# Attention scores taken per head in row tiles and mixed after a trip through DRAM, in place of mixing the queries ahead of the scores

## The chip, the cores and the metric

The kernel runs on one core of a Trainium2 chip. Times are device microseconds of one launch; a launch works through the whole batch of 128 images. The engines are TensorE (PE in the rows; its weight loads are PEld), VectorE (DVE), ScalarE (ACT), GpSimd (POOL) and SyncE (SP), which issues all DMAs here. Less is better.

## The reference, cut to what matters

An image has 384 channels on 14x14 = 196 pixels. After a group normalisation and three 1x1 convolutions there are 8 heads with 32 query and key channels each and 128 value channels each. What the change touches is the talking-heads attention:

```python
attn = jnp.einsum('bhid,bhjd->bhij', q, k) * SCALE        # 8 heads, 196 x 196
attn = attn + ab[:, BIAS_IDXS][None]
attn = jnp.einsum('bhij,gh->bgij', attn, th1w) + _c(th1b)  # mix the heads
attn = jax.nn.softmax(attn, axis=-1)
attn = jnp.einsum('bhij,gh->bgij', attn, th2w) + _c(th2b)  # mix them again
o = jnp.einsum('bhij,bhjd->bhid', attn, v)
o = o.transpose(0, 1, 3, 2).reshape(Bb, DH, RES, RES) + vl # vl: 3x3 depthwise conv of v
o = jax.nn.relu(o)
return conv1x1_bn(o, pw, pb, p_s, p_t)                     # 1024 -> 384 channels
```

The result is added to x. All is float32.

## The kernel before, in words

The batch is worked off in 64 pairs of images. Every engine has one program, written out by hand in its order; `rounds` runs `step` for the first pair, in a loop over the 62 pairs between, and for the last pair. Semaphores tie the engines together; `wait_ge(s, n)` waits until semaphore s has reached n. The projection of one pair to the output lies in the step of the next pair.

Two kinds of matmul occur. `split3` takes operands that were split into a high and a low part and does three matmuls in the one-pass format float32r (low weights by high data, high by low, high by high). Plain float32 matmuls are one instruction in the program and two matmuls (with two weight loads) in the trace.

TensorE does in a step, in this order: 12 tiles `qkv_tile` (values 0 and 1, queries 0 and 1, keys 0 and 1, values 2 to 7) of nine float32r matmuls 128x392, which alternate between the two banks of `psA` and are taken out by ScalarE (`values`, `query_or_key`); projection tiles 0 and 1 of the pair before (`project`, 24 matmuls each); the scores; projection tile 2; the second mixing of the heads (14 uses of `mix_bank`, 4 float32 matmuls each, with `probs` as weights and `mixw` as data); and attention by values (32 float32 matmuls 128x196, image 0 first, then image 1).

The first mixing is folded into the queries: for each of the 8 mixed heads g, ScalarE multiplies the 256 query channels by th1w[g, h] (`mixed_high`, 16 a pair, written to `q_hi`), and VectorE makes the low part (`mixed_low`, 16 a pair, `q_lo`). ScalarE and GpSimd split the keys too (`key_high`, `k_hi`, `k_lo`). One query row of 14 pixels then gives 8 x 14 = 112 weight columns, and the logits of a step are 28 rows x 2 channel tiles x 3 = 168 float32r matmuls of 196 columns, in 14 groups of two rows, each in one of the four banks of `psL` and `psM` (`logit_bank`). VectorE adds the bias and takes the row's greatest value (28 times), ScalarE takes the exponential and the sum (28 times), VectorE the reciprocal of the sums once per image (`rinv`), and GpSimd scales the second mixing matrix by it (`mixing_weights`, four instructions per image).

The values are turned by VectorE (`turn`), go to DRAM in eight DMAs (`turned_out`), come back by key in four (`keys_in`), and are put in the order of the heads by ScalarE (`head_major`, four copies). VectorE's remaining time goes to the depthwise convolution (64 instructions `conv` a pair, dealt out by `convs(count)`), to the adds of convolution and attention (8) and to the low halves of the projection's input (`low`, 8).

## Time and profile before

| what | value |
|---|---|
| median of 3 runs | 4535.83 us (4534.75 to 4536.31) |
| the profiled execution | 4534.58 us |
| its span, first to last instruction | 4532.8 us |
| PE busy | 4505.5 us, 99% |
| DVE busy | 4197.4 us, 93% |
| ACT busy | 3570.3 us, 79% |
| POOL busy | 1360.9 us, 30% |
| one pair in the middle of the run | 70.26 us |
| DMA share of 16 engines | 27.3%, 356 MB in all |

The span is 1.8 us below the profiled execution's time, which is 1.3 us below the median. A busy share says how long an engine had an instruction in it; matmuls are pipelined, so their listed lengths overlap, and what one costs is read from the distance of two starts or from a stretch divided by their count.

### The profile page before, as it was taken

The numbers are of one execution on the slowest core, as the hardware profiler recorded it, in microseconds if no ns is written. First come the engines' busy times: TensorE is split into PE (matmuls) and PEld (weight loads), VectorE is DVE, ScalarE is ACT, GpSimd is POOL, SyncE is SP. The second block draws the span as 40 slices with busy tenths as digits, with TensorE's granted clock in tenths as the row PEclk, the third lists the DMA queues.
The fourth block names the chain that finished last, engine by engine and source line by source line (L and its number), as shares of the span: only waits on it lengthen the run. The fifth ranks groups of instructions, "written<-read, shape, count | busy, mean of one in ns | idle before, by whom it ended". The sixth has DMA issues, their size and how long they took to land.

```text
span 4532.8 us, 108461 instructions
## 1 busy us (share of the span) xinstructions
PE 4505.5 (99%) x33666; PEld 4502.5 (99%) x33666; DVE 4197.4 (93%) x10015; ACT 3570.3 (79%) x8508; POOL 1360.9 (30%) x1288
## 2 busy tenths in 40 slices
PE   7999999999999999999999999999999999999999
PEld 7999999999999999999999999999999999999999
DVE  8999999999999999999999999999999999999998
ACT  7787877878778787787787877878778778787786
POOL 2323323323233232332322323323233232332322
PEclk9999999999999999999999999999999999999999
DMA  3322222223222232222322322223222232232222
GB/s 94 97 65 81 86 69 87 65 81 92 70 81 74 72 97 65 81 82 68 93 65 81 88 72 82 68 78 97 65 81 79 67 97 65 81 86 68 88 65 76
DMA packets 211502, 356.05 MB, mean 79 GB/s; under 512 B 15843, under 2 KB 132691, under 8 KB 211413
## 3 DMA queue, kind: packets, MB, share of 16 engines
q1 hardware_dynamic: 211478, 355.75, 27.3%
q8 instruction: 13, 0.21, 0.0%
q14 instruction: 11, 0.09, 0.0%
HBM read 199.71 MB, written 155.98 MB: 78 GB/s over the span
## 4 chain that ended last, share of the span: by engine, by line
PE 99%; DMA 0%; POOL 0%; DVE 0%; SPq 0%; ACT 0%; issue 0%; POOLq 0%; DVEq 0%
PE psA L293 45%; PE psA L426 15%; PE psL L293 13%; PE psM L293 10%; PE psM L404 9%; PE psL L404 7%; PE psA L306 0%; DMA qa<-in_wqkv 0%; SPq L254 0%; POOL xs L822 0%; DVE probs L730 0%; DMA by_key<-probs 0%; POOL wp_lo L863 0%; DVE q_lo L722 0%; ACT w_hi L443 0%
## 5 line engine op out<-in xcount | busy, mean ns | idle before, releaser
L700 DVE SCALAR_TENSOR_TENSOR psC<-vpad,par,psC 128x406 f32<-128x406 f32 x3072 | 1807.2, 635 | 0.0
L584 ACT ACTIVATE probs<-probs,nmax 112x196 f32<-112x196 f32 x1792 | 803.2, 451 | 128.8 <-DVE nmax L759 112.9
L293 PE MATMUL psA<-x_hi,w_lo 128*128 128x392 f32 x2304 | 794.9, 345 | 6.0 <-DVE x_lo L679 6.0
L293 PE MATMUL psA<-x_hi,w_hi 128*128 128x392 f32 x2304 | 785.7, 341 | 0.0
L293 PE MATMUL psA<-x_lo,w_hi 128*128 128x392 f32 x2304 | 785.1, 341 | 0.0
L426 PE MATMUL psA<-qa,shared 105*128 105x196 f32 x4096 | 690.9, 329 | 0.0
L426 PEld LDWEIGHTS psA<-qa,shared 105*128 105x128 f32 x4096 | 677.2, 190 | 0.4 <-DVE shared L794 0.3
L857 POOL TENSOR_TENSOR k_lo<-qk,k_hi 128x392 fp32r<-128x392 f32 x128 | 159.9, 1249 | 1636.4 <-ACT k_hi L490 1636.4
L722 DVE SCALAR_TENSOR_TENSOR q_lo<-qk,th,q_hi 128x392 fp32r<-128x392 f32 x1024 | 618.3, 632 | 2.0 <-ACT q_hi L486 1.9
L486 ACT ACTIVATE q_hi<-qk,th 128x392 fp32r<-128x392 f32 x1024 | 594.5, 618 | 2.1
L461 ACT ACTIVATE o_hi<-shared 128x392 fp32r<-128x392 f32 x512 | 271.6, 530 | 391.3 <-DVE shared L794 391.3
L293 PE MATMUL psL<-k_hi,q_lo 128*112 128x196 f32 x2048 | 534.4, 261 | 5.3 <-DVE q_lo L722 4.2
L293 PE MATMUL psL<-k_lo,q_hi 128*112 128x196 f32 x2048 | 536.2, 262 | 0.0
L293 PE MATMUL psL<-k_hi,q_hi 128*112 128x196 f32 x2048 | 535.9, 262 | 0.0
L293 PE MATMUL psA<-o_hi,wp_lo 128*128 128x392 f32 x1536 | 526.6, 343 | 0.0
L293 PE MATMUL psA<-o_lo,wp_hi 128*128 128x392 f32 x1536 | 523.1, 341 | 0.0
L293 PE MATMUL psA<-o_hi,wp_hi 128*128 128x392 f32 x1536 | 521.0, 339 | 0.0
L844 POOL TENSOR_TENSOR mixw<-kron,rinv 112x448 f32<-112x448 f32 (+1 forms) x512 | 455.9, 921 | 135.5 <-DVE rinv L773 123.3
L510 ACT ACTIVATE vpad<-psA,par 128x392 f32<-128x392 f32 x512 | 349.5, 683 | 141.6 <-PE psA L293 135.0
L700 DVE SCALAR_TENSOR_TENSOR psC<-vpad,par,shared 128x406 f32<-128x406 f32 x512 | 327.4, 661 | 143.0 <-ACT shared L456 143.0
L293 PEld LDWEIGHTS psA<-x_hi,w_lo 128*128 128x128 f32 x2304 | 434.3, 189 | 6.4 <-issue 6.4
L404 PE MATMUL psM<-mixw,probs 113*105 113x112 f32 x4096 | 435.9, 260 | 4.6 <-POOL mixw L844 4.6
(85 smaller groups left out, 10723.1 us busy)
## 6 DMA issues: line engine op xcount, KB each, us to landing
by_key<-probs SPq DMA_DIRECT2D x512, 224.0 KB, 3.6
qa<-by_key SPq DMA_DIRECT2D x128, 448.0 KB, 4.3
qk<-by_key SPq DMA_DIRECT2D x128, 448.0 KB, 6.9
xs<-in_x SPq DMA_DIRECT2D x64, 588.0 KB, 3.8
shared<-in_x SPq DMA_DIRECT2D x64, 588.0 KB, 3.8
out<-shared SPq DMA_DIRECT2D x63, 588.0 KB, 3.0
qa<-in_wqkv SPq DMA_DIRECT2D x3, 768.0 KB, 7.1
stage_wp<-in_wp SPq DMA_DIRECT2D x1, 1536.0 KB, 9.6
```

Source lines behind the costliest of these rows:

```text
L293: last = nc.tensor.matmul(dst, w, r, start=(begin and n == 0), stop=(end and n == 2))
L404: mm = nc.tensor.matmul(bank[:, jc, :, b, :], probs[0:HP + 1, img, 2 * n + b, jc * HALF:(jc + 1) * HALF], mixw[0:HP + 1, img, 2 * n + b, : ...
L426: mm = nc.tensor.matmul(psA[:, u % 2, e * PIX:(e + 1) * PIX], vt[0:HALF, img, jc, g * D:(g + 1) * D], attn[:, img, jc, g, :], start=(jc == ...
L461: nc.scalar.activation(o_hi[:, 2 * n:2 * n + 2, img * PIX:(img + 1) * PIX], acc[:, 2 * n:2 * n + 2, img * IMG:img * IMG + PIX], ACT.Relu). ...
L486: nc.scalar.activation(q_hi[dst], src, ACT.Copy, scale=th1[:, kt, g:g + 1]).then_inc(s_qhi, 1)
L510: nc.scalar.activation(dst[:, :, 0:RES, 0:RES], psA[:, m % 2, 0:COLS].rearrange("p (i r w) -> p i r w", i=2, w=RES), ACT.Identity, bias=qk ...
L584: nc.scalar.activation(row, row, ACT.Exp, bias=nmax[:, img, b:b + 1], scale=-1.0, accum_out=rowsum[:, img, b:b + 1]).then_inc(s_exp, 1)
L700: nc.vector.scalar_tensor_tensor(a if tap == 7 else sums, src, taps[:, c, TAPS[tap]:TAPS[tap] + 1], a if tap == 0 else sums, MUL, ADD).the ...
L722: nc.vector.scalar_tensor_tensor(q_lo[dst], src, th1[:, kt, g:g + 1], q_hi[dst].bitcast(f32), MUL, SUB).then_inc(s_qlo, 1)
L844: nc.gpsimd.tensor_tensor(mixw[0:HP, img, b0:b0 + nb, :], k2, rinv[:, img, b0:b0 + nb].unsqueeze(2).broadcast_to([HP, nb, HP]), MUL).then_ ...
L857: nc.gpsimd.tensor_tensor(k_lo[:, kt, :], k[:, kt, :], k_hi[:, kt, :].bitcast(f32), SUB).then_inc(s_klo, 1)
```

## The change

The queries are no longer mixed ahead of the scores. A pair's scores are taken per head, in 4 units of 98 query pixels (7 query rows of 14; two units per image). For a unit `head_scores` issues 8 float32 matmuls with only 32 partitions of weights and data each: r is the quarter of the partitions that a head's 32 channels lie in, and the four quarters write to the four banks of `psL` and `psM`. The units stand on TensorE's queue behind value tiles 2, 3, 4 and 5. ScalarE copies two banks and VectorE two banks of each unit into `scores`; SP stores the unit to DRAM (`scores_out`) and loads it back with one partition per head and pixel column (`heads_in`) into `by_head`: 8 transfers a pair. The first mixing is then one float32 matmul of 392 columns for two query rows, 14 a pair, with the constant matrix `kron1` as weights. These stand in fours ahead of the projection tiles. The splits of queries and keys and the weight table `th1` go away. The order of attention by values becomes image by image within each pair of heads and starts only when all 14 mixing uses were copied; ReLU is done twice (once into `o_hi`, once in place); six of the eight low halves go to GpSimd, and so do two of the four `head_major` copies.

```diff
+        scores = qa[0:UNIT, :].rearrange("p (i c h n) -> p i c h n", i=2, c=2, h=NH)
+        turned = qa[:, 0:TURNED].rearrange("p (i b c n) -> p i b c n", i=2, b=BLOCKS, c=VT)
+        head_rows = nc.dram_tensor("head_rows", (4, NH, UNIT, PIX), f32, kind="Internal").ap()
+        raw = [v.rearrange("p (j n) -> p j n", j=2) for v in (qa[:, TURNED:TURNED + 2 * DH], qk_room[:, 0:2 * DH])]
...
-        def mixed(kt, g):
-
-            return ((slice(None), slice(None), kt, slice(g * RES, (g + 1) * RES)),
-                    q[:, kt, :].rearrange("p (b i) -> p b i", i=RES))
-
+        def score_bank(r):
+
+            return (psL if r < 2 else psM)[:, r % 2, 0:2 * PIX]
+
+        UNITS = [(img, c) for img in range(2) for c in range(2)]
...
+            def scores_out(t, u):
+
+                img, c = UNITS[u]
+                sp.wait_ge(s_score_a, 8 * t + 2 * u + 2)
+                sp.wait_ge(s_score_v, 8 * t + 2 * u + 2)
+                sp.dma_start(head_rows[u].rearrange("h i j -> i h j"), scores[0:UNIT, img, c, :, :]
+                             ).then_inc(s_score_out[u], 16)
+
+            def heads_in(t, u):
+
+                img, c = UNITS[u]
+                sp.wait_ge(s_score_out[u], 16 * (t + 1))
+                sp.dma_start(by_head[:, img, c * ROWS_B * PIX:(c + 1) * ROWS_B * PIX],
+                             head_rows[u].rearrange("h (w b) j -> (h w) (b j)", w=RES)).then_inc(s_moved[u], 16)
...
-                turned_out(t)
-                ones_in(t)
-                keys_in(t)
+                if first:
+                    sp.wait_ge(s_bias, 1)
+                else:
+                    wait_alone(sp, s_olo, 6 * t)
+                    wait_alone(sp, s_olo_v, 2 * t)
+                    wait_alone(sp, s_av_mm, 8 * t)
+                scores_out(t, 0)
+                scores_out(t, 1)
+                heads_in(t, 0)
+                scores_out(t, 2)
+                heads_in(t, 1)
+                scores_out(t, 3)
+                heads_in(t, 2)
+                heads_in(t, 3)
+                turned_out(t, 0)
+                turned_out(t, 1)
+                keys_in(t, 0)
+                keys_in(t, 1)
...
+            def head_scores(t, first, u):
+
+                img, c = UNITS[u]
+                if u:
+                    pe.wait_ge(s_score_a, 8 * t + 2 * u)
+                    pe.wait_ge(s_score_v, 8 * t + 2 * u)
+                else:
+                    pe.wait_ge(s_qk_sb, 4 * t + 4)
+                    if not first:
+                        pe.wait_ge(s_mix_sb, 14 * t)
+                at_ = (2 * img + c) * UNIT
+                for kt in range(QT):
+                    for r in range(QUADS):
+                        part_ = slice(r * KD, (r + 1) * KD)
+                        mm = nc.tensor.matmul(score_bank(r)[0:UNIT, kt * PIX:(kt + 1) * PIX],
+                                              q[part_, kt, at_:at_ + UNIT],
+                                              k[part_, kt, img * PIX:(img + 1) * PIX], start=True, stop=True)
+                mm.then_inc(s_score_mm, 1)
...
+                    if m < 6:
+                        head_scores(t, first, m - 2)
                 if first:
                     pe.wait_ge(s_v_sb, VT)
-                else:
-                    project(t, 0, True)
-                    project(t, 1, True)
-
-                pe.wait_ge(s_klo, 2 * (t + 1))
-                pe.wait_ge(s_qlo, 16 * (t + 1))
...
+                    if n == 0:
+                        pe.wait_ge(s_score_a, 8 * t + 8)
+                        pe.wait_ge(s_score_v, 8 * t + 8)
+                    if n % 7 == 0:
+                        pe.wait_ge(s_moved[2 * img], MOVES * (t + 1))
+                    if n % 7 == 3:
+                        pe.wait_ge(s_moved[2 * img + 1], MOVES * (t + 1))
...
-                    elif not first:
-                        pe.wait_ge(s_mix_sb, 14 * (t - 1) + 11 + n)
-                    for b in (b0, b0 + 1):
-                        for kt in range(QT):
-                            px = slice(img * PIX, (img + 1) * PIX)
-                            mm = split3(logit_bank(n)[:, (b - b0) * PIX:(b - b0 + 1) * PIX],
-                                        q_lo[:, img * RES + b, kt, :], q_hi[:, img * RES + b, kt, :],
-                                        k_lo[:, kt, px], k_hi[:, kt, px], kt == 0, kt == QT - 1)
-                    mm.then_inc(s_logit_mm, 1)
+                    nc.tensor.matmul(logit_bank(n)[:, 0:2 * PIX], kron1[:, :, :].rearrange("p g i -> p (g i)"),
+                                     by_head[:, img, b0 * PIX:(b0 + 2) * PIX], start=True, stop=True
+                                     ).then_inc(s_logit_mm, 1)
...
+                    if n in (3, 7, 11) and not first:
+                        if n == 7 and not last:
+                            pe.wait_ge(s_gs, t + 2)
+                        project(t, n // 4, True)
+
+                if first:
...
                 for img in range(2):
-                    pe.wait_ge(s_vt_sb, 4 * t + 2 * img + 2)
-                    pe.wait_ge(s_mix_sb, 14 * t + 7 * img + 7)
-                    for n in range(4):
-                        u = 4 * img + n
-                        if u >= 2:
-                            pe.wait_ge(s_add, 8 * t + u - 1)
...
+                    pe.wait_ge(s_vt_sb[img], 2 * (t + 1))
+                pe.wait_ge(s_mix_sb, 14 * t + 14)
+                for u in range(8):
+                    n, img = divmod(u, 2)
+                    if u >= 2:
+                        pe.wait_ge(s_add, 8 * t + u - 1)
...
-            def relu(t, img, n):
-                act.wait_ge(s_add, 8 * t + 4 * img + n + 1)
-                nc.scalar.activation(o_hi[:, 2 * n:2 * n + 2, img * PIX:(img + 1) * PIX],
-                                     acc[:, 2 * n:2 * n + 2, img * IMG:img * IMG + PIX], ACT.Relu).then_inc(s_relu, 1)
...
+            def relu(t, u):
+                n, img = divmod(u, 2)
+                act.wait_ge(s_add, 8 * t + u + 1)
+                a = acc[:, 2 * n:2 * n + 2, img * IMG:img * IMG + PIX]
+                nc.scalar.activation(o_hi[:, 2 * n:2 * n + 2, img * PIX:(img + 1) * PIX], a, ACT.Relu).then_inc(s_relu, 1)
+                nc.scalar.activation(a, a, ACT.Relu).then_inc(s_relu, 1)
...
-            def mixed_high(t, kt, g):
-                act.wait_ge(s_qk_sb, 4 * t + kt + 1)
-                dst, src = mixed(kt, g)
-                nc.scalar.activation(q_hi[dst], src, ACT.Copy, scale=th1[:, kt, g:g + 1]).then_inc(s_qhi, 1)
-
-            def key_high(t, kt):
-                act.wait_ge(s_qk_sb, 4 * t + kt + 3)
-                nc.scalar.copy(k_hi[:, kt, :], k[:, kt, :]).then_inc(s_khi, 1)
-
-            def head_major(t, img, jc):
-                act.wait_ge(s_raw[img], 32 * (t + 1))
-                nc.scalar.copy(vt[0:HALF, img, jc, :].rearrange("p (c a n) -> p c a n", c=VT, a=QUADS),
-                               raw[img][0:HALF, jc, :].rearrange("p (a c n) -> p c a n", a=QUADS, c=VT)
-                               ).then_inc(s_vt_sb, 1)
...
+            def head_major(t, jc):
+                act.wait_ge(s_raw[1], 32 * (t + 1))
+                nc.scalar.copy(vt[0:HALF, 1, jc, :].rearrange("p (c a n) -> p c a n", c=VT, a=QUADS),
+                               raw[1][0:HALF, jc, :].rearrange("p (a c n) -> p c a n", a=QUADS, c=VT)
+                               ).then_inc(s_vt_sb[1], 1)
...
+                for u in range(4):
+                    values(2 + u)
+                    score_copy(t, u, 0)
+                    score_copy(t, u, 1)
+                    if u < 2:
+                        conv_centre(t, first, u + 2)
+                    elif not last:
+                        stat(t + 1, 0, u - 2)
...
-                CENTRES = {1: 4, 3: 5, 9: 6, 11: 7}
+                CENTRES = {8: 4, 11: 5, 23: 6, 25: 7}
...
+                    if n == 3 and not last:
                         group_moments(t + 1)
                     if n in CENTRES:
-                        conv_centre(t, CENTRES[n])
+                        conv_centre(t, first, CENTRES[n])
+                    if n in (7, 15) and not first:
+                        projected(t, n // 8)
                 if not first:
                     projected(t, 2)
...
+                    if use == 0:
+                        act.wait_ge(s_vt_out[0], OUTS * (t + 1))
+                        act.wait_ge(s_vt_out[1], OUTS * (t + 1))
+                        act.wait_ge(s_moved[2], MOVES * (t + 1))
                     if use == 7:
-                        act.wait_ge(s_vt_sb, 4 * t + 2)
+                        act.wait_ge(s_moved[3], MOVES * (t + 1))
+                        act.wait_ge(s_vt_sb[0], 2 * (t + 1))
...
-                    if use in COPIES:
-                        head_major(t, *COPIES[use])
-                    if use == 6 and not last:
+                    if use in (3, 6):
+                        head_major(t, use // 4)
+                if not first:
+                    act.wait_ge(s_proj_mm, 3 * t)
+                for u in range(8):
+                    relu(t, u)
+                    if u == 0 and not last:
                         act.wait_ge(s_v_mm, VT * (t + 1))
                         x_high(t + 1)
...
+                def score_copies(u):
+                    img, c = UNITS[u]
+                    dve.wait_ge(s_score_mm, 4 * t + u + 1)
+                    for r in (2, 3):
+                        nc.vector.tensor_copy(scores[0:UNIT, img, c, r:NH:QUADS, :],
+                                              score_bank(r)[0:UNIT, :].rearrange("p (k n) -> p k n", k=QT)
+                                              ).then_inc(s_score_v, 1)
...
+                convs(14)
+                if first:
+                    dve.wait_ge(s_wlo, CT)
+                for u in range(4):
+                    score_copies(u)
+                    convs(2 if u < 3 else 3)
...
+                    if n in (3, 7):
+                        turn(n // 4)
+                        convs(3)
+                    if n == 11:
+                        convs(7)
...
+            def head_major(t, jc):
+
+                if jc == 0:
+                    wait_alone(pool, s_logit_mm, 14 * t + 11)
+                wait_alone(pool, s_raw[0], 32 * (t + 1))
+                nc.gpsimd.tensor_copy(vt[0:HALF, 0, jc, :].rearrange("p (c a n) -> p c a n", c=VT, a=QUADS),
+                                      raw[0][0:HALF, jc, :].rearrange("p (a c n) -> p c a n", a=QUADS, c=VT)
+                                      ).then_inc(s_vt_sb[0], 1)
...
                 mixing_weights(t, first, 0)
+                head_major(t, 0)
+                head_major(t, 1)
                 mixing_weights(t, first, 1)
                 if not first:
                     residual(t, 2)
```

TensorE's queue at the end of the projection tiles and the start of the logits, kernel before (x_hi, o_hi and the like are high parts, the second name is the weight):

```order
L293 MATMUL psA<-o_hi,wp_hi 128x392
L369 REGISTER_ALU
L370 REGISTER_ALU [waits s_klo]
L376 ISA [waits s_qlo]
L293 MATMUL psL<-k_hi,q_lo 112x196 [waits s_mix_sb]
L293 MATMUL psL<-k_lo,q_hi 112x196
L293 MATMUL psL<-k_hi,q_hi 112x196
```

The logits follow behind projection tile 1 and wait for the split keys and queries. In the changed kernel the first of four groups of scores stands right behind value tile 2:

```order
L371 REGISTER_ALU [waits s_qk_sb]
L376 MATMUL psL<-qk_room 98x196 [waits s_mix_sb]
L376 MATMUL psL<-qk_room 98x196
L376 MATMUL psM<-qk_room 98x196 x2
L376 MATMUL psL<-qk_room 98x196 x2
L376 MATMUL psM<-qk_room 98x196 x2
L320 MATMUL psA<-x_hi,w_lo 128x392 [waits s_qk_sb]
```

It waits for the last key tile, and value tile 3 follows. The logits of the changed kernel stand behind value tile 7; projection tile 0 (L320, o_hi) follows behind the fourth:

```order
L420 REGISTER_ALU [waits s_score_v,s_score_a]
L425 MATMUL psL<-shared,kron 112x392 [waits s_moved0]
L425 MATMUL psL<-shared,kron 112x392
L425 MATMUL psM<-shared,kron 112x392
L429 REGISTER_ALU
L430 REGISTER_ALU [waits s_v_sb]
L333 MATMUL psA<-mv,same 128x4 [waits s_stat]
L425 MATMUL psM<-shared,kron 112x392 [waits s_moved1]
L339 REGISTER_ALU
L346 ISA [waits s_v_sb]
L320 MATMUL psA<-o_hi,wp_lo 128x392 [waits s_olo]
```

What was 12 matmuls a group is one, and the waits are now for the loads back from DRAM (s_moved0, s_moved1). SP's queue in the loop, before, behind the load of x:

```order
L254 DMA by_key<-probs 32x7x256 [waits s_turned]
L254 DMA by_key<-probs 32x7x256 x7
L259 REGISTER_ALU
L260 DMA probs<-in_ones 1x3584 [waits s_vt_out]
L264 REGISTER_ALU
L267 DMA qa<-by_key 112x1024 [waits s_logit_mm]
L267 DMA qa<-by_key 112x1024
L267 DMA qk<-by_key 112x1024 x2
```

And in the changed kernel, at the same place, with L262 `scores_out` and L269 `heads_in`:

```order
L262 DMA head_rows<-qa 98x8x196 [waits s_score_v,s_score_a]
L260 REGISTER_ALU
L262 DMA head_rows<-qa 98x8x196 [waits s_score_v,s_score_a]
L268 REGISTER_ALU
L269 DMA shared<-head_rows 112x1372 [waits s_score_out0]
L260 REGISTER_ALU
L262 DMA head_rows<-qa 98x8x196 [waits s_score_v,s_score_a]
L269 DMA shared<-head_rows 112x1372 [waits s_score_out1]
L260 REGISTER_ALU
L262 DMA head_rows<-qa 98x8x196 [waits s_score_v,s_score_a]
L269 DMA shared<-head_rows 112x1372 [waits s_score_out2]
L269 DMA shared<-head_rows 112x1372 [waits s_score_out3]
```

The eight stores of the turned values, which were first, follow behind the last of these rows.

## Rows read from the trace of the kernel before

**Rows 1.** Windows, one pair by stage: length, busy (x instructions) per engine, PEclk, DMA share, GB/s

```profile
1985.88:2005.30 19.42, 19.42 (x111) 19.42 (x109) 16.76 (x29) 16.07 (x28) 2.50 (x2) 1.00 0.00 0
2005.30:2013.87 8.57, 8.57 (x49) 8.57 (x49) 8.57 (x14) 7.87 (x17) 0.00 (x0) 1.00 0.42 97
2013.87:2030.60 16.73, 16.73 (x171) 16.73 (x170) 16.41 (x69) 14.66 (x55) 10.17 (x10) 1.00 0.21 61
2030.60:2034.92 4.32, 4.32 (x27) 4.31 (x26) 4.32 (x12) 1.71 (x8) 2.36 (x4) 1.00 0.75 221
2034.92:2045.65 10.73, 10.73 (x113) 10.73 (x112) 10.73 (x21) 10.21 (x18) 6.18 (x6) 1.00 0.63 194
2045.65:2056.14 10.49, 10.49 (x66) 10.49 (x65) 8.59 (x17) 5.18 (x10) 0.00 (x0) 1.00 0.19 57
1985.88:2056.14 70.26, 70.26 (x528) 70.24 (x527) 65.39 (x157) 55.69 (x134) 21.20 (x20) 1.00 0.27 78
```

**Rows 2.** The page, part 1: busy time and share of the span

```profile
PE 4505.5 (99%) x33666; PEld 4502.5 (99%) x33666; DVE 4197.4 (93%) x10015; ACT 3570.3 (79%) x8508; POOL 1360.9 (30%) x1288
```

**Rows 3.** Groups of PE by form: busy us, mean ns of one | idle before

```profile
L426 PE MATMUL psA<-qa,shared 105*128 105x196 f32 x4096 | 690.9, 329 | 0.0
```

**Rows 4.** Timeline of PE: start us, length us, instruction (merged rows as x)

```profile
2017.40 0.30 PE L306 MATMUL psA<-mv,same 128*128 128x4 f32 x2
2017.56 0.33 PE L293 MATMUL psM<-k_hi,q_lo 128*112 128x196 f32 x1
...
2056.14 0.48 PE L293 MATMUL psA<-x_hi,w_lo 128*128 128x392 f32 x1
2056.46 0.34 PE L293 MATMUL psA<-x_lo,w_hi 128*128 128x392 f32 x1
2056.64 0.34 PE L293 MATMUL psA<-x_hi,w_hi 128*128 128x392 f32 x1
```

**Rows 5.** Timeline of ACT in the attention-mixing stage

```profile
2038.03 0.97 ACT L601 COPY qa<-psL 105x448 f32<-105x448 f32 x2
...
2045.36 1.03 ACT L601 COPY qa<-psM 105x448 f32<-105x448 f32 x2
```

**Rows 6.** Groups of DVE by form

```profile
L722 DVE SCALAR_TENSOR_TENSOR q_lo<-qk,th,q_hi 128x392 fp32r<-128x392 f32 x1024 | 618.3, 632 | 2.0 <-ACT q_hi L486 1.9
...
L794 DVE TENSOR_TENSOR shared<-psA,shared 128x392 f32<-128x392 f32 x512 | 289.6, 566 | 140.0 <-PE psA L426 140.0
```

**Rows 7.** Groups of ACT by form

```profile
L584 ACT ACTIVATE probs<-probs,nmax 112x196 f32<-112x196 f32 x1792 | 803.2, 451 | 128.8 <-DVE nmax L759 112.9
L486 ACT ACTIVATE q_hi<-qk,th 128x392 fp32r<-128x392 f32 x1024 | 594.5, 618 | 2.1
...
L461 ACT ACTIVATE o_hi<-shared 128x392 fp32r<-128x392 f32 x512 | 271.6, 530 | 391.3 <-DVE shared L794 391.3
L601 ACT COPY qa<-psM 105x448 f32<-105x448 f32 x512 | 263.3, 557 | 24.5 <-PE psM L404 18.8
...
L494 ACT COPY shared<-qa 105x1024 f32<-105x1024 f32 x128 | 135.4, 1058 | 0.0
```

**Rows 8.** Groups of POOL by form

```profile
L844 POOL TENSOR_TENSOR mixw<-kron,rinv 112x448 f32<-112x448 f32 x384 | 389.4, 1041 | 135.5 <-DVE rinv L773 123.3 <-DVE rinv L769 12.2
...
L827 POOL TENSOR_TENSOR x_lo<-xs,x_hi 128x1176 fp32r<-128x1176 f32 x63 | 169.7, 2694 | 255.1 <-ACT x_hi L439 255.1
```

**Rows 9.** The page, part 6: DMA issues, KB each, us to landing

```profile
by_key<-probs SPq DMA_DIRECT2D x512, 224.0 KB, 3.6
qa<-by_key SPq DMA_DIRECT2D x128, 448.0 KB, 4.3
```

**Rows 10.** Timeline of SP's queue: the eight stores of the turned values

```profile
2009.29 6.30 SPq L254 DMA_DIRECT2D by_key<-probs  x8
```

**Rows 11.** Windows of the value stores and of the loads back, columns as in Rows 1

```profile
2009.00:2018.50 9.50, 9.50 (x76) 9.49 (x75) 9.37 (x27) 7.79 (x22) 0.00 (x0) 1.00 0.74 193
2030.80:2041.00 10.20, 10.20 (x88) 10.19 (x88) 10.20 (x24) 7.06 (x17) 5.65 (x7) 1.00 0.80 238
```

292 lines of the change are left out of this document (118 added, 174 removed).

## Prediction

> **What bounds the kernel now.** I read the page's busy shares first: PE 99%, DVE 93% [rows 2]. A share alone would not decide it, so I cut one pair of the middle of the run into TensorE's stages with the windows view [rows 1]. In each of the six stages PE is busy for the whole stretch, at full granted clock, and the stages add up to the pair: 19.42 + 8.57 + 16.73 + 4.32 + 10.73 + 10.49 = 70.26 us. DVE is busy 65.39 us of it, ACT 55.69, POOL 21.20. So the time of the pair is what stands on TensorE's queue, and the other engines hide behind it. 64 pairs of 70.26 are 4497 us; the other 36 are the start, and the projection of the last pair. Below, T is the time since the pair's first value tile (1985.88 in the trace). The projection begins at T = 19.42, the second mixing (10.73) at 49.04, attention by values at 59.77.
>
> **What leaves TensorE.** The logits stretch, 16.73 us. The two small group-sum matmuls in it stay; they take 0.16, from one start to the next [rows 4]. That leaves 16.57 us, or 0.0986 per float32r matmul of 196 columns (168 of them).
>
> **What comes, the mixing.** A float32 matmul shows as two, each over twice the columns' time: attention by values has 32 in the code and 64 per pair in the trace (4096 of 64 pairs, [rows 3]), in 10.49 us [rows 1], 0.164 each at 196 columns. The new mixing has 14 matmuls of 392 columns, 28 halves of 2 x 0.164 = 0.328: 9.18 us.
>
> **What comes, the scores.** 32 float32 matmuls of 196 columns are 64 halves. No row shows matmuls on 32 partitions, so the cost is bounded by the nearest row, the same 0.164. If the four quarters of the array do not overlap at all: 64 x 0.164 = 10.49. If four run abreast all the time: 2.62. The code's order decides between them. The quarters follow one another, but each matmul's two halves use the same quarter, so the second half has to wait for the first; if starts stay in the queue's order, the next quarter starts only with that second half. Then two run abreast: 9 steps of 0.164 a unit, 1.48, and 5.90 a pair. I take this one. No row here shows either.
>
> The array changes eight times a pair between whole and quarters. Unseen too: at least nothing, at most about 0.37 a change, the difference of a matmul's listed length and its pitch (0.34 - 0.18 [rows 4]) plus a load of some 0.2. I take 0.14, what the pitch grows by when PE goes from attention to the split matmuls (56.14 to 56.46 is 0.32, the next pitch 0.18, [rows 4]): 1.12. The same 0.14 three times for the returns from the mixing's groups to the projection: 0.42. "TensorEngine Tiling (Array Packing)", Key Properties, in the Trainium skill says that a change of tiling mode drains the engine; the price is left open there.
>
> The sum on TensorE: 9.18 + 5.90 + 1.12 + 0.42 = 16.62 in, 16.57 out. **The work is a draw**; what decides is the new waits.
>
> **Wait 1, ahead of attention by values.** Before, image 0 needed only the first seven copied mixing uses, and attention began where the mixing ended [rows 1]. Now it waits for the copy of the last use. ScalarE's copies follow each other in about 0.49 (two in 0.97 to 1.03, [rows 5], 0.557 alone [rows 7]); with the hand-over on both sides I take 0.65. Nothing is left on PE's queue to cover it.
>
> **Wait 2, in the mixing.** Projection tile 2 stood between the logits and the mixing; now the last two logit groups come behind it, and mixing use 0 follows them directly. ScalarE still has the last four exponentials (0.451 each), one convolution centre and the copy of tile 2 ahead of its first mixing copy, some 3.3 us after the last group, while PE has four banks = 3.07 us of mixing before it needs one back. Then two `head_major` copies of 1.058 [rows 7] stand in the first seven uses. I take 0.4.
>
> **Wait 3, the scores' trip through DRAM.** A tile takes 19.42 / 12 = 1.62. Value tile 2 is the seventh and ends at T = 11.3, unit 0 some 1.6 later, at 12.9; it is copied at 14.0 (two copies of 0.56 each on ScalarE and VectorE, [rows 6, 7]). A unit is 98 x 8 x 784 bytes = 615 KB each way. The stores of the turned values, in runs of 1 KB, moved 193 GB/s at 0.74 of the engines, so 261 at full share; the loads back, in runs of 4 KB, 238 at 0.80, so 298 [rows 11]. With runs of 784 bytes and 98 partitions I estimate 2.9 us a store, and 2.1 a load, each with about 1.3 until the semaphore (a 224 KB store lands after 3.6, a 448 KB load after 4.3, [rows 9]; issuing one takes SP 6.30 / 8 = 0.79, [rows 10]). Up to the load of unit 1, which the fourth logit group waits for, the queue moves out 0, out 1, in 0, out 2, in 1: 14.5 + 2.9 + 2.9 + 2.1 + 2.9 + 2.1 + 1.3 = 28.7. PE gets there at 19.42 + 7.02 + 2.1 = 28.5. I take 0.3. Units 2 and 3 land by about 36, and their groups are due at 35 and 41, behind projection tiles. So this wait is the floor under any speed-up of the scores: each microsecond that they save brings PE to the fourth group earlier, and the transfers come hardly earlier.
>
> **What lies under cover.** VectorE loses 16 x 0.632 and six `low`, and gains 8 copies of about 0.57: some 9 us freed, off the path. ScalarE loses 16 x 0.618 and two `head_major`, gains 8 copies and 8 ReLUs of 0.530 [rows 7]: slightly less than before. Both have room in the pair's 70 us. `x_high` moves behind the first ReLU: ready 4.2 us after attention starts, x_lo (2.694, [rows 8]) at 6.9, needed at 10.49. If that cover went, the next pair's first tile would be late by the excess. The eight value stores move behind the scores' transfers and behind the second `turn`; they come back by T = 48, and attention needs them at 60.
>
> **Sum.** 0.05 + 0.65 + 0.4 + 0.3 = +1.4 us a pair; x 64 = +90. From the profiled execution's 4534.6 that is **4624 us**, 1.9% slower. Its own range, with the switch between 0 and 0.37 and the waits between half and double, is 4500 to 4715.
>
> **Rivals.**
> 1. Four abreast, but the floor binds: scores 2.62 instead of 5.90, the fourth group due at T = 25.3 and fed at about 28.1. 1.4 - 3.3 + 2.5 = +0.6 a pair: 4573. For it: the order of starts is only assumed. Chance 0.13.
> 2. **The other side: faster.** Four abreast, and the transfers quick enough (the DMA engines are idle at share 0.00 in the first 19 us, [rows 1]): 1.4 - 3.3 - 0.3 = -2.2 a pair: 4394. It decides when scores, changes and wait 3 together stay below 5.9 us instead of my 7.3. Against it: 1.9 MB of stores and loads between T = 14 and 28. Chance 0.18.
> 3. No overlap of the quarters: 10.49 instead of 5.90, wait 3 gone, +5.7 a pair: 4899. Chance 0.12.
> 4. GpSimd late: `head_major` of image 0 stands ahead of image 1's mixing weights on its queue and waits for the load back. If a copy of 1024 elements goes like x_lo (2.694 for 1176), two take 4.7, from T = 48 to 53, then the first weights 1.041 [rows 8]; use 7 is due at 55. A load 2.5 us later costs +1.5: 4720. Chance 0.12.
>
> **How the numbers follow.** The forecast has 0.45; of it 0.06 falls below the time before and 0.05 within 0.2% of it, about what a measurement of this kernel can tell from no change. Faster: 0.18 + 0.06 + 0.03 of rival 1 = 0.27; same: 0.05 + 0.04 = 0.09; slower 0.64. The range goes from rival 2's middle, 4395, to 4800 above rival 4: out stay rival 3 (0.12) and rival 2's better half.
>
> **What would show it.** The starts of the L376 matmuls: 0.164 between a quarter's halves and the next quarter's start with the second half; a unit near 1.5 us (0.7 or 2.7 in the rivals). Mixing halves at 0.328. PE's waits by name: the fourth logit group on the load of unit 1, attention's first matmul on ScalarE's last copy, mixing uses 4 and 7. PE's share falls to some 98%. Wrong it would be if DMA waits stand at other groups, or if ScalarE holds up value tiles 3 to 5 (2.5 us of its work a unit against 3.1 on PE).

## The result, and the profile after

| kernel | median, us | span of the profiled execution, us |
|---|---|---|
| before | 4535.29 (4 runs) | 4532.8 |
| changed | 4592.5 (4587.41 to 4595.26, 4 runs) | 4593.4 |

The changed kernel takes 1.0125 times as long, 95% interval 1.0113 to 1.0137: 57 us more. The forecast was 4624, range 4395 to 4800. (Of the experiments, one has only two timed runs: two others were disturbed and are left out.)

The page of the changed kernel, part 1 and the DMA queue of part 3 (packets, MB, share of 16 engines):

```profile
PE 4377.9 (95%) x28802; PEld 3920.6 (85%) x28802; DVE 3787.2 (82%) x9120; ACT 3322.5 (72%) x8252; POOL 1661.4 (36%) x1672
q1 hardware_dynamic: 448262, 669.57, 51.0%
```

Against [rows 2], TensorE has less to do (4377.9 us instead of 4505.5) in a longer span; VectorE and ScalarE have less too. No engine is full. So the question is what TensorE waits for. Its waits in the changed kernel, the view of who waited for whom (total us, times, longest), of which the kernel before had none that came back every pair:

```profile
PE psM L425 <- DMA shared<-head_rows: 87.4, 65, 2.1
PE psM L449 <- ACT qa L635: 42.5, 64, 1.8
PE psA L471 <- ACT qa L635: 40.0, 64, 0.7
PE psA L320 <- DVE shared L818: 20.3, 64, 0.4
PE psA L333 <- DVE mv L691: 7.0, 1, 7.0
PE psA L320 <- DVE x_lo L714: 5.9, 1, 5.9
PE psL L425 <- DVE nmax L778: 3.8, 2, 2.9
```

The first four come once a pair: 1.37 us for the load of unit 1 at the fourth logit group, 0.66 in the second mixing for ScalarE's copies, 0.63 for ScalarE's last copy ahead of attention, and 0.32 at the first value tile for an add of VectorE; 2.97 us together. The last three are the start of the run; the first two of them, of 7.0 and 5.9 us, were there before.

One pair of the changed kernel in four stages, windows view with the columns of [rows 1]: tiles and scores, logits with the three projection tiles, second mixing, attention.

```profile
2010.47:2034.12 23.65, 23.65 (x173) 21.59 (x173) 18.62 (x34) 18.38 (x33) 0.61 (x1) 1.00 0.36 100
2034.12:2057.86 23.74, 22.46 (x104) 18.14 (x103) 19.63 (x65) 15.56 (x57) 11.48 (x12) 1.00 0.83 233
2057.86:2070.26 12.40, 11.14 (x113) 10.78 (x111) 12.32 (x30) 11.30 (x26) 6.20 (x7) 1.00 0.34 105
2070.26:2081.46 11.20, 10.88 (x65) 10.58 (x65) 8.42 (x16) 6.58 (x14) 7.58 (x7) 1.00 0.33 106
```

The pair takes 70.99 us against 70.26 [rows 1]. The stages say where. Tiles and scores are 23.65 against 19.42 for the tiles alone: scores and array changes cost 4.23. Logits and projection were 16.73 + 8.57 + 4.32 = 29.62 and are 23.74, with a wait of 1.28 inside. The mixing grew from 10.73 to 12.40, with two waits of 0.64 and 0.62 (the second is the one ahead of attention), and the rest, 0.41, lies behind the waits: TensorE has no weights loaded ahead there and starts more slowly. Attention grew from 10.49 to 11.20, of it 0.31 the wait of the next pair's first tile; of the other 0.40, some 0.24 is again such a slower start. Over all pairs of the loop but four the mean is 71.04 us against 70.27 before, 48 us in 62 pairs.

**Four pairs are different: TensorE's clock fell in them.** A window of one of them, with the columns of [rows 1], and the timeline of TensorE at its start:

```profile
3035.80:3039.20 3.40, 3.40 (x11) 3.08 (x10) 2.54 (x6) 0.99 (x4) 3.22 (x3) 0.50 0.71 202
```

```profile
3035.30 1.20 PE L425 MATMUL psM<-shared,kron 112*112 112x392 f32 x2 [2.12 <-DMA shared<-head_rows]
3035.75 1.08 PE L320 MATMUL psA<-o_hi,wp_lo 128*128 128x392 f32 x1
3036.63 0.53 PE L320 MATMUL psA<-o_lo,wp_hi 128*128 128x392 f32 x1
3036.96 0.53 PE L320 MATMUL psA<-o_hi,wp_hi 128*128 128x392 f32 x1
```

A granted clock of 0.50 is 1.2 GHz, and the projection's matmuls follow each other in 0.33 us there where they take 0.18 otherwise. The four pairs take 73.0 to 73.4 us, so this costs 9 us. Each of the four falls came behind a wait of 1.64 to 2.12 us for the load of unit 1; other waits of that length passed without one. In the kernel before, the clock doesn't fall in the loop. The first pair adds 2 us (77.1 against 74.8) and the stretch behind the last pair's start 2 us: together 61, the difference of the two spans; the medians differ by 57.

The score matmuls of one unit between value tiles 2 and 3, timeline of TensorE of the changed kernel (start us, length us; x2 are two quarters of the array):

```profile
2021.66 0.34 PE L320 MATMUL psA<-x_hi,w_hi 128*128 128x392 f32 x1
2021.94 0.41 PE L376 MATMUL psL<-qk_room 32*98 32x196 f32 x2
2021.95 0.41 PE L376 MATMUL psM<-qk_room 32*98 32x196 f32 x2
2022.18 0.33 PE L376 MATMUL psL<-qk_room 32*98 32x196 f32 x2
2022.19 0.33 PE L376 MATMUL psM<-qk_room 32*98 32x196 f32 x2
...
2022.51 0.33 PE L376 MATMUL psL<-qk_room 32*98 32x196 f32 x2
2022.53 0.33 PE L376 MATMUL psM<-qk_room 32*98 32x196 f32 x2
2022.79 0.44 PE L320 MATMUL psA<-x_hi,w_lo 128*128 128x392 f32 x1
```

A matmul of each quarter, a half of it, starts within 0.02 us of the others, and the next four halves start 0.16 to 0.24 later: four run abreast all the time, not two. From the end of the last tile's pitch (2021.66 + 0.18) to the next tile are 0.95 us, and the next tile's first pitch is 0.28 instead of 0.18 (2022.79 to 2023.07): 1.05 a unit.

The trip through DRAM, timeline of SP's queue of the same pair (start us, length of issuing):

```profile
2024.05 3.01 SPq L262 DMA_DIRECT2D head_rows<-qa  x2
2028.14 0.32 SPq L269 DMA_DIRECT2D shared<-head_rows  x1
2029.38 0.31 SPq L262 DMA_DIRECT2D head_rows<-qa  x1
2031.13 0.32 SPq L269 DMA_DIRECT2D shared<-head_rows  x1
2032.04 0.85 SPq L262 DMA_DIRECT2D head_rows<-qa  x1
2035.70 4.38 SPq L269 DMA_DIRECT2D shared<-head_rows  x2
```

The store of unit 0 has landed 4.1 us after its issue (its load starts at 2028.14; 4.2 was forecast). The load of unit 1 is issued at 2031.13 and its data let TensorE go on at 2037.65, 6.5 us later, while the median of the four loads of a pair is 5.8. The store of unit 2 was issued 1.75 us ahead of it and the store of unit 3 0.9 behind it. In 2034.12 to 2037.65 the DMA engines are at share 0.97.

### The profile page after: what moved, and what is told of

The parts are those of the page before. It is cut to its first block, busy times and chain, and to the rows that moved or that the text cites. A ratio compares the mean times of both kernels' runs of the same rounds, so it can differ in the third digit from the quotient of the medians.

```text
span 4593.4 us, 99947 instructions
## 1 busy us (share of the span) xinstructions
PE 4377.9 (95%) x28802; PEld 3920.6 (85%) x28802; DVE 3787.2 (82%) x9120; ACT 3322.5 (72%) x8252; POOL 1661.4 (36%) x1672
## 4 chain that ended last, share of the span: by engine, by line
PE 66%; DMA 16%; issue 7%; DVE 6%; ACT 4%; DVEq 0%; ACTq 0%; SPq 0%; POOLq 0%
PE psA L320 31%; PE psA L471 13%; DMA shared<-head_rows 9%; PE psM L449 7%; DMA head_rows<-qa 6%; PE psM L425 5%; PE psL L449 4%; PE psL L425 4%; PE psL L376 2%; ACT probs L614 2%; DVE psC L735 2%; ACT qa L635 1%; DVE shared L735 1%; DVE qa L751 1%; DVE shared L818 1%
## 5 line engine op out<-in xcount | busy, mean ns | idle before, releaser
L735 DVE SCALAR_TENSOR_TENSOR psC<-vpad,par,psC 128x406 f32<-128x406 f32 x3072 | 1764.9, 634 | 0.0
L320 PE MATMUL psA<-x_hi,w_lo 128*128 128x392 f32 x2304 | 822.3, 357 | 25.9 <-DVE shared L818 20.0
L320 PE MATMUL psA<-x_hi,w_hi 128*128 128x392 f32 x2304 | 786.6, 341 | 0.0
L320 PE MATMUL psA<-x_lo,w_hi 128*128 128x392 f32 x2304 | 786.6, 341 | 0.0
L471 PE MATMUL psA<-qa,shared 105*128 105x196 f32 x4096 | 696.3, 331 | 40.0 <-ACT qa L635 40.0
L471 PEld LDWEIGHTS psA<-qa,shared 105*128 105x128 f32 x4096 | 677.0, 190 | 51.5 <-ACT qa L635 49.7
L320 PE MATMUL psA<-o_hi,wp_lo 128*128 128x392 f32 x1536 | 585.2, 381 | 0.3 <-DVE shared L818 0.3
L868 POOL TENSOR_TENSOR o_lo<-shared,o_hi 128x392 fp32r<-128x392 f32 x384 | 354.8, 953 | 541.8 <-ACT shared L511 533.3
L320 PEld LDWEIGHTS psA<-x_hi,w_lo 128*128 128x128 f32 x2304 | 432.8, 188 | 110.9 <-ACT vpad L555 49.3
L320 PE MATMUL psA<-o_lo,wp_hi 128*128 128x392 f32 x1536 | 525.6, 342 | 0.0
L320 PE MATMUL psA<-o_hi,wp_hi 128*128 128x392 f32 x1536 | 523.7, 341 | 0.0
L449 PE MATMUL psM<-mixw,probs 113*105 113x112 f32 x4096 | 442.2, 261 | 45.1 <-ACT qa L635 42.5
L449 PEld LDWEIGHTS psM<-mixw,probs 113*105 113x105 f32 x4096 | 418.1, 172 | 77.5 <-ACT qa L635 54.1
L778 DVE CUSTOM_DVE_ANT_0 probs<-psL,bias 112x196 f32<-112x196 f32 x1024 | 323.4, 358 | 194.8 <-PE psL L425 193.5
L735 DVE SCALAR_TENSOR_TENSOR psC<-vpad,par,shared 128x406 f32<-128x406 f32 x512 | 371.8, 748 | 128.6 <-ACT shared L503 127.3
L887 POOL TENSOR_TENSOR mixw<-kron,rinv 112x448 f32<-112x448 f32 (+1 forms) x512 | 436.2, 883 | 77.9 <-DVE rinv L793 71.8
L818 DVE TENSOR_TENSOR shared<-psA,shared 128x392 f32<-128x392 f32 x512 | 284.0, 565 | 183.7 <-PE psA L471 175.2
L320 PEld LDWEIGHTS psA<-x_lo,w_hi 128*128 128x128 f32 x2304 | 434.6, 189 | 0.3 <-issue 0.3
```

Of the source, the lines that this page charges most:

```text
L320: last = nc.tensor.matmul(dst, w, r, start=(begin and n == 0), stop=(end and n == 2))
L449: mm = nc.tensor.matmul(bank[:, jc, :, b, :], probs[0:HP + 1, img, 2 * n + b, jc * HALF:(jc + 1) * HALF], mixw[0:HP + 1, img, 2 * n + b, : ...
L471: mm = nc.tensor.matmul(psA[:, u % 2, e * PIX:(e + 1) * PIX], vt[0:HALF, img, jc, g * D:(g + 1) * D], attn[:, img, jc, g, :], start=(jc == ...
L735: nc.vector.scalar_tensor_tensor(a if tap == 7 else sums, src, taps[:, c, TAPS[tap]:TAPS[tap] + 1], a if tap == 0 else sums, MUL, ADD).the ...
L778: nc.vector.tensor_tensor_reduce(out=keys(img, b), in0=logit_bank(n)[:, (r % 2) * PIX:(r % 2 + 1) * PIX].rearrange("p (r w) -> p r w", w=RES),
L818: nc.vector.tensor_tensor(a, psA[:, u % 2, 0:COLS].rearrange("p (c n) -> p c n", c=2), a, ADD).then_inc(s_add, 1)
```

## The experiments

Each kernel is the changed one with one edit, unless it says otherwise; ratios are to the kernel before, run on the same chip.

**Do the starts keep the queue's order?**

```diff
-                for kt in range(QT):
-                    for r in range(QUADS):
+                for r in range(QUADS):
+                    for kt in range(QT):
```

> Changed kernel with the loops over quarter and channel tile exchanged: both matmuls of a quarter follow each other on the queue. Theory A (starts keep the queue's order, as the prediction assumed): the next quarter starts only with the last of the four halves of the one before, 13 steps of 0.164 a unit = 2.1 us instead of the 0.85 seen; +5.1 us a pair, of which 1.3 are taken back from the wait for the load of unit 1: about 4830 us. Theory B (every quarter has a queue of its own and starts when it is free): a unit stays at 0.85 us, 4592 us.

Measured: 4610.13 us, ratio 1.0169 (1.0152 to 1.0186). Theory A is off by 220 us; theory B is nearly right, with 18 us on top. About 10 of the 18 are the clock: it fell nine times in the loop of that profiled execution, four times in the changed kernel's. The pairs in which it did not fall take 71.17 us against 71.04, which makes the other 8. The timeline of TensorE in that kernel:

```profile
2028.93 0.42 PE L376 MATMUL psL<-qk_room 32*98 32x196 f32 x2
2028.96 0.42 PE L376 MATMUL psM<-qk_room 32*98 32x196 f32 x2
2029.18 0.34 PE L376 MATMUL psL<-qk_room 32*98 32x196 f32 x2
2029.20 0.34 PE L376 MATMUL psM<-qk_room 32*98 32x196 f32 x2
```

psM belongs to the third and fourth quarter, which stand behind four matmuls of the first two in the code; they start 0.03 us after the first. So in both orders a quarter started when it was free, whatever stood ahead of it for another quarter. Coming later on the queue costs the third quarter 0.02 to 0.03 us, where it was 0.01 in the changed kernel.

**What would two abreast have cost?** The unit's matmuls issued twice.

```diff
-                for kt in range(QT):
+                for kt in range(2 * QT):
+                    kt %= QT
```

> Changed kernel that issues every unit's eight score matmuls twice (same result), so that a unit costs what two abreast would cost: +0.66 us a unit, +2.6 a pair on TensorE. Theory of the floor (the transfers of unit 1 start only 1.3 us later, PE arrives 2.6 later, so the wait of 1.37 shrinks to about 0.1): +1.3 us a pair, 4675 us. Rival (the matmul time counts in full and the wait stays): +2.6, 4757 us.

Measured: 4710.91 us, ratio 1.0386 (1.0370 to 1.0402), 118 us above the changed kernel or 1.85 a pair: between the two. In its trace a unit takes 1.6 us and the wait at the fourth group fell by half:

```profile
PE psM L426 <- DMA shared<-head_rows: 44.7, 56, 1.7
```

87.4 - 44.7 = 42.7 us, 0.67 a pair, against the 2.6 of the matmuls: the floor gives back a quarter, since the doubled units also delay the transfers behind them. The clock did not fall in the loop of this kernel, which is another 9 us given back: 64 x (2.6 - 0.67) - 9 = 115. A unit of 1.6 us is also near the forecast's own picture of the scores (7.02 / 4 = 1.75), and with it the kernel takes 87 us more than the forecast's sum. So that sum had the waits too low while it had the scores too high.

**Is the wait for unit 1 a queue or a latency?**

```diff
-                scores_out(t, 2)
                 heads_in(t, 1)
+                scores_out(t, 2)
```

> Changed kernel with the load of unit 1 issued ahead of the store of unit 2. Theory (the transfers queue: the load of unit 1 took 6.5 us because the stores of units 2 and 3 shared the engines with it): it lands some 1.5 to 2 us earlier, the wait of 1.37 us a pair at the fourth logit group nearly goes, 4505 to 4520 us. Rival (the length is the fixed latency of a store and a load in a row): no change at that wait, 4590 us. Second rival: the later store of unit 2 makes a new wait at the eighth group, 4550 or more.

Measured: 4506.73 us, ratio 0.9938 (0.9922 to 0.9955): 86 us less for two lines exchanged, and faster than the kernel before. It was not a fixed latency. The wait is down to

```profile
PE psM L425 <- DMA shared<-head_rows: 10.3, 17, 3.6
```

and the loads land after a median of 4.7 us instead of 5.8. The timeline of SP's queue of one pair, whose first value tile starts at 1973.09:

```profile
1986.67 3.01 SPq L262 DMA_DIRECT2D head_rows<-qa  x2
1990.76 3.24 SPq L269 DMA_DIRECT2D shared<-head_rows  x2
1994.17 0.89 SPq L262 DMA_DIRECT2D head_rows<-qa  x2
```

The load of unit 1 is not issued earlier: it still waits for its own store, and goes out 20.8 us after the pair's first tile, 20.7 in the changed kernel (medians). What moved is the store of unit 2, from 18.9 to 21.3, behind the load. The load of unit 1 then lands 4.6 us after its issue instead of 6.5. So what held it up was the store of unit 2 moving at the same time, not its own issue. Of the 86 us 77 are the wait; the clock did not fall in the loop of this kernel, and that is the other 9. The later store of unit 2 made no wait at the eighth group.

**Covering the wait with projection tile 0.**

```diff
-                    if n in (3, 7, 11) and not first:
+                    if n in (2, 7, 11) and not first:
...
-                        project(t, n // 4, True)
+                        project(t, (2, 7, 11).index(n), True)
```

> Changed kernel with projection tile 0 ahead of the fourth logit group instead of behind it. Theory (the wait of 1.37 us a pair for the load of unit 1 is bare because nothing stands ahead of it, and the 4.3 us of tile 0 cover it): the wait goes, 63 x 1.37 = 86 us less, 4506 us, and no other wait on TensorE grows by more than 0.2 us a pair. Rival (the softmax chain on VectorE and ScalarE gets its fourth group of rows later and hands the time back in the mixing): 4560 to 4595, with the wait for ScalarE's copies in the mixing grown from 0.66 us a pair to over 1.2.

Measured: 4630.25 us, ratio 1.0209 (1.0192 to 1.0226), 38 us slower than the changed kernel: my theory fell. TensorE's waits there:

```profile
PE psM L449 <- ACT qa L635: 90.9, 63, 1.4
PE psL L449 <- DVE nmax L778: 71.8, 63, 1.2
PE psA L471 <- ACT qa L635: 40.0, 64, 0.7
```

The wait for the load is down to 1.3 us in all, as meant, and 72 + 48 us came in the mixing, where the last rows' greatest values now arrive late. VectorE waited for the fourth group 64 times, 285.6 us in all, and had its `turn` and three convolutions (2.04 + 3 x 0.55 = 3.7 us) only behind it. If that is the cause, they must move with the tile:

```diff
-                    if n in (3, 7):
+                    if n in (2, 7):
                         turn(n // 4)
```

> As the kernel with projection tile 0 ahead of the fourth logit group, and VectorE's first turn with its three convolutions behind group 2 instead of group 3. Theory (that kernel lost because VectorE stood 4.5 us idle for the fourth group and did the turn and the convolutions, 3.7 us, only behind it, so that the last rows came late for the mixing): VectorE does them in the idle time, the waits in the mixing fall back to 0.66 us a pair and the wait for the load of unit 1 stays away: 4500 to 4520 us. Rival (the loss is in the order of the logit groups itself): 4600 or more.

Measured: 4491.51 us, ratio 0.9905 (0.9889 to 0.9922). 139 us between two places of one `turn`. TensorE's waits of this kernel:

```profile
PE psM L449 <- ACT qa L635: 41.6, 64, 1.0
...
PE psM L425 <- DMA shared<-head_rows: 3.5, 3, 1.6
```

The wait for the load is nearly gone, the wait for `nmax` too, and the mixing's wait for ScalarE is back at 0.65 a pair. The clock did not fall in the loop of either kernel. So tile 0 does cover the wait for the load, if VectorE's `turn` comes with it.

**Attention gated by image.** The first unit of attention is one of image 0; it then waits only for the first seven copied uses, and the second, of image 1, for all 14.

```diff
-                for img in range(2):
-                    pe.wait_ge(s_vt_sb[img], 2 * (t + 1))
-                pe.wait_ge(s_mix_sb, 14 * t + 14)
                 for u in range(8):
                     n, img = divmod(u, 2)
+                    if n == 0:
+                        pe.wait_ge(s_vt_sb[img], 2 * (t + 1))
+                        pe.wait_ge(s_mix_sb, 14 * t + 7 * (img + 1))
```

> Changed kernel, where attention's first unit waits only for image 0's seven mixing copies and the second for all 14. Theory (the 0.63 us a pair ahead of attention is the last copy, bare, and the first unit's 1.31 us cover it): the wait goes, 63 x 0.63 = 40 us less, up to 60 if the restart behind the wait (10.88 us of attention instead of 10.49) goes too: 4535 to 4552. Rival (the time comes back at the first value tile of the next pair, which waits for VectorE's add): 4585 to 4592.

Measured: 4542.91 us (10 runs, 4537.84 to 4551.08), ratio 1.0021 (1.0012 to 1.0031), 50 us less. The wait at L471 is gone from the list, and the others stand nearly where they were:

```profile
PE psM L425 <- DMA shared<-head_rows: 90.3, 65, 2.4
PE psM L449 <- ACT qa L635: 41.6, 64, 0.9
```

40 of the 50 us are the wait. The other 10 are in no row of waits. In the changed kernel the first weight load of attention starts together with the first matmul, behind the wait; without the wait it starts 0.09 us ahead of it, under the last matmul of the mixing. That is 0.25 us a pair until the second matmul, and 3 us in all come back at the wait for the load, 90.3 instead of 87.4.

**Projection tile 2 taken off the mixing's first copy.** ScalarE's copy of that tile moves into its loop over the logits, behind row 23.

```diff
-                    if n in (7, 15) and not first:
+                    if n in (7, 15, 23) and not first:
                         projected(t, n // 8)
-                if not first:
-                    projected(t, 2)
```

> Changed kernel, where ScalarE copies projection tile 2 out behind the exponential of row 23 (ahead of those of the last four rows) instead of behind that of row 27. Theory (ScalarE reaches the first mixing copy too late by about this copy's 0.68 us): the wait of 0.66 us a pair at the fifth mixing use goes, 63 x 0.66 = 42 us less, 4545 to 4555 us. Rival (the wait is for the mixing copies' own pace of 0.49 to 0.77 us a use, not for the copy ahead of them): over 4575.

Measured: 4558.65 us (4 runs), ratio 1.0053 (1.0038 to 1.0068), 34 us less. The wait at L449 for ScalarE, 42.5 us, is gone from the list; the rest of TensorE's waits are unchanged (87.7, 40.0 and 20.3). So what made ScalarE late there was the tile's copy, which stood behind the last exponentials. The end moved by 8 us less than the wait was long. They stayed at the same place, below what the list of waits shows. TensorE's timeline in this kernel, two mixing uses a row:

```profile
2045.33 1.70 PE L449 MATMUL psL<-mixw,probs 113*105 113x112 f32 x16
2047.11 1.78 PE L449 MATMUL psM<-mixw,probs 113*105 113x112 f32 x16
2048.72 1.70 PE L449 MATMUL psL<-mixw,probs 113*105 113x112 f32 x16
```

Two uses take 1.53 us where nothing holds them. Here the fifth use comes 1.78 behind the third, and the seventh 1.61 behind the fifth: 0.33 us a pair are left.

**VectorE's convolutions spread.** The rest of the convolutions stood ahead of the add of unit 6, on which the next pair's first value tile waits.

```diff
-                    if u == 6:
-                        convs(64)
...
-                    convs(1)
+                    convs(2 if u in (3, 4) else 1)
```

> Changed kernel, where VectorE does the last two convolution instructions behind the adds of units 3 and 4 instead of both ahead of the add of unit 6. Theory (the first value tile of the next pair waits 0.32 us for the add of unit 6, late by two instructions of 0.55): the wait goes, 63 x 0.32 = 20 us less, 4572 us. Rival (that add waits for attention's matmuls anyway): 4590.

Measured: 4561.95 and 4563.62 in two runs, 30 us less. The wait at L320 for VectorE, 20.3 us, is gone from the list of waits. Since two runs give no interval, the same kernel was run again:

> The same kernel as the one with VectorE's last two convolutions moved ahead, of whose four timed runs two were disturbed: 4563 us, as its two undisturbed runs (4561.95 and 4563.62), 29 us below the changed kernel: 20 for the wait and 9 for the restart behind it.

Measured: 4572.7 us (4566.05 to 4576.47), ratio 1.0082 (1.0065 to 1.0099), 20 us less than the changed kernel, where the two runs had 30. The two profiled executions show what lies between them: in the loop the clock fell five times in the first and eight times in the second. The pairs in which it did not fall take 70.60 us in both, against 71.04. So at equal clock the edit is worth 0.44 us a pair, 28 us: 20 are the wait, and the slower start behind it goes too.

**Do the terms add?** The four edits together: the load of unit 1 first, attention by image, tile 2 early, the convolutions spread.

> Changed kernel with the load of unit 1 ahead of the store of unit 2, attention gated by image, tile 2 copied out early and the convolutions moved ahead. If the four waits are independent terms of one sum, as the prediction has them: 4592 - 86 - 50 - 42 - 20 = 4394 us, 3.1% below the kernel before. Rival (they cover each other, since taking one away brings TensorE earlier to the next): 4430 to 4480.

Measured: 4382.57 us (4379.13 to 4385.24, 5 runs), ratio 0.9664 (0.9651 to 0.9677). That is 210 us less than the changed kernel, where the single edits gave 86 + 50 + 34 + 20 to 30 = 190 to 200, and 3.4% less than the kernel before. Of the 210, 9 are the clock, which did not fall in the loop here. In the pairs at full clock the single edits give 1.24 + 0.80 + 0.56 + 0.44 = 3.04 us and the four together 3.19: the terms add. Its page, part 1, the longest of its waits in total, and one pair in the windows view:

```profile
PE 4342.2 (99%) x28802; PEld 3905.2 (89%) x28802; DVE 3780.4 (86%) x9120; ACT 3329.4 (76%) x8252; POOL 1662.7 (38%) x1672
```

```profile
PE psM L425 <- DMA shared<-head_rows: 9.8, 13, 3.9
```

```profile
1984.78:2052.46 67.68, 67.60 (x453) 60.93 (x452) 58.87 (x142) 51.92 (x130) 25.94 (x27) 1.00 0.54 153
```

TensorE is busy 67.60 of the pair's 67.68 us: here it is the bound again, as before the change, and the pair is 2.58 us shorter than the 70.26 of [rows 1]. The work as measured in the changed kernel gives 4.23 + 9.24 + 0.1 - 16.57 = -3.0; of the 0.4 between them 0.16 lies in attention, which takes 10.65 us here and 10.49 in [rows 1], and the 0.33 that the edit of tile 2 left lies in the mixing, 11.06 against 10.73. The arithmetic of the change is a gain, and its waits had turned it into a loss.

## Why the prediction was right or wrong

The direction and the range were right: 1.3% slower against 1.9% forecast. But the sum came near by errors that met. Scores and array changes were priced 2.8 us a pair too high. The floor of the text gave only 1.1 of them back, at wait 3. Wait 2 gave 0.3, and 1.2 came from terms that the sum did not have: 0.3 at the first value tile, 0.8 of slower work in the mixing and attention, 0.1 for the clock. Without these the kernel would have been some 0.3 us a pair faster than the one before, so that the direction came out right was luck too.

**The score matmuls: the step that failed.** "Then two run abreast ... 5.90 a pair. I take this one." Together with the array changes that was 7.02; measured are 4.23. The starts don't stay in the queue's order for matmuls of different quarters, and the order by quarters, which should have cost most, adds 18 us, 10 of them the clock (the first experiment). The row that I took for the scores, float32 halves of 0.164, was right; the rule for their overlap was not. I named the other order as a rival and gave it too little, because the sentence of "TensorE: Matmul & The Clock Gate", Part 3, fitted my reading. The Trainium skill speaks there of packed matmuls in general; for these, float32 with two halves on 32 partitions, the measurement differs and decides. Its 3.07 for four row tiles is given for 512 columns and no type stands there, so "bf16" was mine; here 10.49 became 4.23 with the array changes, 2.5 times.

**The array changes.** Forecast 1.12 for eight. A unit costs 1.05 in all; four halves of each quarter at 0.164 are 0.66 of it, so 0.39 is left for two changes and the drain of the last quarter, 1.56 a pair. The bound of 0.37 for a change held, 0.14 was low; with the overlap right the two terms would have been 2.62 + 1.56.

**The mixing.** Forecast 28 x 0.328 = 9.18, measured 28 x 0.33 = 9.24. **The returns to the projection**: 0.42 forecast; from the end of the logit halves, at 0.33 each, to the next group the three tiles take 4.38, 4.28 and 4.29 against 4.285, so 0.1.

**Wait 1**: 0.65 forecast, 0.63 measured, and 0.25 more behind it, which the forecast did not have. **Wait 2**: 0.4 forecast, 0.66 measured, at use 4 and for the reason forecast; at use 7, the other place named, TensorE did not wait.

**Wait 3.** 0.3 forecast, 1.37 measured. The transfers were estimated well (unit 0 landed 4.1 us after its issue, 4.2 forecast). In the pair shown the group is due at T = 25.9 and is fed at 27.2, where the forecast had 28.5 and 28.7. TensorE came 2.6 us early and the load 1.5. That is the floor of the text, and the mechanism of rival 1: four abreast, and the floor binds. Rival 1 gave 4573 us for 4592.5, with a wait of 2.8 us, twice the one measured, and with nothing for what follows the waits. Undoing the earliness with doubled scores halved the wait; exchanging two transfers took it away. This wait also cost the 9 us of the clock, at which the forecast did not look: the falls came only in kernels that have it nearly in full.

**Unforeseen.** The first value tile waits 0.32 for an add of VectorE behind the remaining convolutions. I had looked at that place only for `x_low`. And TensorE starts slower behind each wait, 0.25 a pair at wait 1.

**The rivals.** Rival 2, faster, needed scores, changes and wait 3 below 5.9 us together; they were 4.23 + 1.37 = 5.60. The condition was met, the other waits ate it: they sum to 1.61, where 1.05 was forecast, and the pair has 0.4 more in attention and 0.4 in the mixing, most of it behind waits. Rival 4 did not happen; GpSimd's copy is as quick as ScalarE's, in the groups of the changed kernel:

```profile
L875 POOL COPY shared<-qa 105x1024 f32<-105x1024 f32 x128 | 129.4, 1039 | 170.9 <-DMA qa<-by_key 170.9
```

ScalarE did not hold up the value tiles either: no wait for it stands at them.

## What to carry to other kernels

When a change lets the bounding engine do less, work out the waits at the new, earlier due times before pricing the work: here 3 us of work saved a pair became 0.7 lost, since four waits of 0.3 to 1.4 us were uncovered, and a wait cost more than its length: 0.25 us for the slower start at one of them, and the clock at the longest. For a wait on a transfer, ask first what else is moving at that time: issuing one store behind a load instead of ahead of it gave 86 us, more than any other edit to the changed kernel alone. Where two runs of one kernel differ, look at the granted clock before looking for a cause in the code. And when work moves to cover a wait, move with it what other engines do behind it: the same projection tile gave 38 us more, and with VectorE's `turn` 101 us less than the changed kernel.

## What the runs showed of the hardware that was not expected

- Float32 matmuls on four quarters of the array ran four abreast in both orders tried: in the order by quarters the third quarter started 0.03 us after the first with four matmuls between them. A unit of 8 (16 halves of 196 columns) takes 0.95 us with what it costs to change the array, and 1.05 with the longer first pitch behind it.
- TensorE's granted clock fell to 1.2 GHz in the middle of a run, behind single short waits. In the six traces with the wait for the load of unit 1 nearly in full (the changed kernel, the order by quarters, attention by image, tile 2 early, and the convolutions twice) it fell 33 times in the loop, each time behind such a wait, of 1.6 to 2.2 us; about as many waits of that length passed without a fall. In the kernel before and in the five kernels in which that wait is halved or nearly gone it never fell there.
- An evacuation by ScalarE of the same 128 x 392 tile takes 1.12 us where the queries are written permuted and 0.68 where the keys are not. Timeline of ScalarE in the changed kernel:

```profile
2015.62 1.12 ACT L569 ACTIVATE qk_room<-psA,par 128x392 f32<-128x392 f32 x1 [0.17 <-PE psA L320]
...
2018.83 0.68 ACT L569 ACTIVATE qk_room<-psA,par 128x392 f32<-128x392 f32 x1 [0.48 <-PE psA L320]
```

- The loads of 615 KB took 5.8 us from issue to landing in the median with the load of unit 1 issued behind the store of unit 2, and 4.7 with it ahead; the load of unit 1 itself took 6.5 and 4.6, issued at the same point of the pair.
- GpSimd copies 105 x 1024 float32 in 1.04 us; ScalarE took 1.06 for it in [rows 7].
